# Inverse square roots of the normalizations: ScalarE's Sqrt replaced by a bit-pattern start and three Newton steps on VectorE

## The reference

```
h = layernorm(x) * (1 + ca) + sa;   x = x + ga * mixer(h)
h = layernorm(x) * (1 + cb) + sb;   x = x + gb * experts(h)
layernorm(x) = (x - mean) / sqrt(var + 1e-5)          # over the 256 features
```

## Time and profile before

| | |
|---|---|
| median of 3 runs | 2297.69 us (2289.25 to 2305.37) |
| the profiled execution's own time | 2296.97 us |
| its span in the profile | 2295.2 us |
| PE busy | 1986.1 us, 87% |
| VectorE busy | 1700.5 us, 74% |
| ScalarE busy | 1461.2 us, 64% |
| GpSimd busy | 973.7 us, 42% |
| mean granted TensorE clock | 0.93 of full speed |

### The profile page before, as it was taken

The page is one execution under the profiler, slowest core; times in us unless marked ns, Lnnn a source line. Parts: engine busy times, 40 slices in busy tenths (PEclk is TensorE's granted clock), DMA queues, the critical chain, the costliest instruction groups (busy, mean ns, idle before and its releaser), DMA issues.

```text
span 2295.2 us, 40993 instructions
## 1 busy us (share of the span) xinstructions
PE 1986.1 (87%) x12211; PEld 1622.4 (71%) x12211; DVE 1700.5 (74%) x3913; ACT 1461.2 (64%) x3983; POOL 973.7 (42%) x1025
## 2 busy tenths in 40 slices
PE   4787988887699468999998998999989999689995
PEld 4566766666677256888877887878877788467772
DVE  4676766676634667999899998999989997664444
ACT  1473747465244157888887888878887887345550
POOL 0120302021177112455454765547655567177550
PEclk8799989899699779999999999999999999899998
DMA  4147383837833403444343554445534452635557
GB/s 129 38 152 295 130 350 106 338 109 282 328 97 102 147 10 138 158 154 145 127 147 125 169 175 144 142 137 171 165 137 142 146 179 93 214 117 176 162 146 272
DMA packets 143589, 372.67 MB, mean 162 GB/s; under 512 B 22256, under 2 KB 67696, under 8 KB 141072
## 3 DMA queue, kind: packets, MB, share of 16 engines
q1 hardware_dynamic: 128160, 328.39, 41.8%
q0 software_dynamic: 15216, 41.67, 5.3%
HBM read 232.71 MB, written 137.27 MB: 161 GB/s over the span
## 4 chain that ended last, share of the span: by engine, by line
PE 60%; DVE 17%; ACT 13%; issue 5%; DMA 2%; POOL 1%; SPq 1%; DVEq 0%; POOLq 0%; ACTq 0%
PE bank L2148 12%; PE bank L2204 6%; ACT work L701 5%; PE bank L2585 5%; PE bank L2176 4%; DVE cv L2315 3%; PE bank L2197 3%; PE bank L2189 3%; PE bank L1074 3%; PE bank L2622 2%; ACT l_mat L2239 2%; PE bank L2162 2%; DVE nmax L607 2%; PE bank L1103 2%; PE bank L775 1%
## 5 line engine op out<-in xcount | busy, mean ns | idle before, releaser
L2148 PE MATMUL bank<-h_hi,wi 128*128 128x512 f32 x1024 | 403.9, 436 | 1.3 <-ACTq L151 1.3
L2239 ACT ACTIVATE l_mat<-l_mat,cum_tok 128x128 f32<-128x128 f32 x1024 | 315.1, 424 | 0.0
L2315 DVE SCALAR_TENSOR_TENSOR cv<-bank,cw,cv 128x511 f32<-128x511 f32 (+2 forms) x384 | 287.4, 748 | 32.1 <-ACT cv L2245 13.5
L2368 POOL TENSOR_TENSOR xdec<-xdt,dec_tok 128x384 f32<-128x384 f32 x128 | 107.9, 843 | 387.6 <-DVE xdt L2305 354.4
L2383 POOL TENSOR_TENSOR yg<-yd,sgt 128x512 f32<-128x512 f32 x128 | 227.2, 1775 | 45.7 <-DVE yd L2322 45.7
L2204 PE MATMUL bank<-wo,yg 128*128 128x256 f32 x1024 | 242.5, 380 | 1.5 <-POOL yg L2383 1.5
L2148 PEld LDWEIGHTS bank<-h_hi,wi 128*128 128x128 f32 x1024 | 195.5, 191 | 62.0 <-issue 23.8
L2148 PE MATMUL bank<-h_lo,wi 128*128 128x512 f32 x512 | 203.4, 397 | 0.0
L2204 PEld LDWEIGHTS bank<-wo,yg 128*128 128x128 f32 x1024 | 185.1, 191 | 21.5 <-POOL yg L2383 1.9
L2376 POOL TENSOR_TENSOR gates<-gates,sq 128x512 f32<-128x512 f32 x128 | 164.1, 1282 | 72.0 <-ACT sq L2256 71.9
L845 POOL CAST w_hi<-w_raw 128x512 fp32r<-128x512 f32 x32 | 21.1, 659 | 392.0 <-ACTq L151 241.2
(11 more groups left out here) (419 smaller groups left out, 4947.6 us busy)
## 6 DMA issues: line engine op xcount, KB each, us to landing
sorted_rows<-blank SPq DMA_DIRECT2D x16, 4644.0 KB, 31.9
wi<-in_weights_split SPq DMA_DIRECT2D x128, 512.0 KB, 3.8
l_mat<-running_sums SPq DMA_DIRECT2D x128, 512.0 KB, 4.9
experts_got<-chosen_rows SPq DMA_DIRECT2D x32, 512.0 KB, 8.6
wo<-out_weights_normed SPq DMA_DIRECT2D x128, 128.0 KB
experts_xt<-sorted_rows SPq DMA_DIRECT2D x127, 129.0 KB, 2.3
w_raw<-in_wi SPq DMA_DIRECT2D x32, 256.0 KB, 2.7
in_weights_split<-w_hi SPq DMA_DIRECT2D x32, 256.0 KB, 2.9
```

Source lines behind the costliest of these rows:

```text
L2148: mm = e.matmul(dst[:, :], l, r[:, k, tok], start=(n == 0), stop=(n == 3 * KD - 1))
L2239: last = e.activation(part, part, ACT.Relu, bias=cum_tok[:, c, hh, bass.ds(w.g, 1)], scale=-1.0)
L2315: e.scalar_tensor_tensor(out=cv[:, w.two, n:SEQ], in0=PSX[w.two][:, 0:SEQ - n], scalar=cw[:, bass.ds(w.f, 1), TAPS - 1 - n], in1=cv[:, w.t ...
```

## The change

The wait for ScalarE goes from all five places, with the semaphores for it; `Sqrt` goes from ScalarE, and the two Exps into `warm`. `rsqrt_dve` reads plane 0 as an integer, multiplies it by -0.5 and adds a constant, which gives a first approximation of the inverse root as a bit pattern, and refines it three times with three instructions each: ten dependent instructions where there were five.

```
-        v.e.tensor_scalar(rs[:, 0, 0:TT], mv[:, 0:TT, 1], EPS, None, ALU.add).then_inc(n_var, 1)
-        v.e.wait_ge(n_root, c)
+        v.step(v.e.tensor_scalar(rs[:, 0, 0:TT], mv[:, 0:TT, 1], EPS, None, ALU.add))
         rsqrt_dve(v, TT)
...
     def rsqrt_dve(v, n):
 
-        v.step(v.e.reciprocal(rs[:, 2, 0:n], rs[:, 1, 0:n]))
-        v.step(v.e.tensor_tensor(rs[:, 3, 0:n], rs[:, 0, 0:n], rs[:, 2, 0:n], ALU.mult))
-        v.step(v.e.tensor_tensor(rs[:, 3, 0:n], rs[:, 3, 0:n], rs[:, 2, 0:n], ALU.mult))
-        v.step(v.e.tensor_scalar(rs[:, 3, 0:n], rs[:, 3, 0:n], -0.5, 1.5, ALU.mult, ALU.add))
-        v.step(v.e.tensor_tensor(rs[:, 2, 0:n], rs[:, 2, 0:n], rs[:, 3, 0:n], ALU.mult))
+        v.step(v.e.tensor_scalar(rs[:, 2, 0:n].bitcast(I32), rs[:, 0, 0:n].bitcast(I32), -0.5, ROOT_BITS, ALU.mult,
+                                 ALU.add))
+        for _ in range(3):
+            v.step(v.e.tensor_tensor(rs[:, 3, 0:n], rs[:, 0, 0:n], rs[:, 2, 0:n], ALU.mult))
+            v.step(v.e.scalar_tensor_tensor(out=rs[:, 3, 0:n], in0=rs[:, 3, 0:n], scalar=-0.5, in1=rs[:, 2, 0:n],
+                                            op0=ALU.mult, op1=ALU.mult))
+            v.step(v.e.scalar_tensor_tensor(out=rs[:, 2, 0:n], in0=rs[:, 3, 0:n], scalar=1.5, in1=rs[:, 2, 0:n],
+                                            op0=ALU.add, op1=ALU.mult))
 
     def norm_act(a, b, layer, first=None, last=None):
...
-        a.e.wait_ge(n_var, c)
-        a.e.activation(rs[:, 1, 0:TT], rs[:, 0, 0:TT], ACT.Sqrt).then_inc(n_root, 1)
...
     def route_act(a, r, s, at):
         e = a.e
-        if (s, at) == (0, "m"):
-            e.wait_ge(*q_var(r + 1))
-            e.activation(rs[:, 1, 0:TT], rs[:, 0, 0:TT], ACT.Sqrt).then_inc(q_root.sem, 1)
-            e.activation(warm[:, 1:2], ones_c[:, :], ACT.Exp)
...
-            e.tensor_scalar(rs[:, 0, 0:TT], mv[:, 0:TT, 1], EPS, None, ALU.add).then_inc(q_var.sem, 1)
+            v.own.add(e.tensor_scalar(rs[:, 0, 0:TT], mv[:, 0:TT, 1], EPS, None, ALU.add))
         if (s, at) == (0, "z"):
-            e.wait_ge(*q_root(r + 1))
+            e.wait_ge(s_dve, v.own.now())
             rsqrt_dve(v, TT)
...
-        e.wait_ge(t_var, b + 1)
-        e.activation(rs[:, 1, 0:TT], rs[:, 0, 0:TT], ACT.Sqrt).then_inc(t_root, 1)
-        e.activation(warm[:, 0:1], ones_c[:, :], ACT.Exp)
...
                         ALU.add).then_inc(t_var, 1)
-        e.wait_ge(t_root, b + 1)
+        e.wait_ge(t_var, b + 1)
         rsqrt_dve(v, TT)
```

More of the change, by code:

```diff
@@ L33 @@
 NEG = -3.0e38
+ROOT_BITS = float(0x5F3759DF)
 SSM_HEADS, SSM_P, SSM_N = 64, 64, 128
@@ L186, in program @@
     block = ctx.enter_context(nc.Block())
-    n_var, n_root, n_rows, n_turned, n_high, n_full = (
-        sem("norm_" + n) for n in ("variance", "root", "rows", "turned", "high", "full"))
+    n_rows, n_turned, n_high, n_full = (
+        sem("norm_" + n) for n in ("rows", "turned", "high", "full"))
     def norm_dve(v, b, layer, before=None, meanwhile=None, last=None):
@@ L948, in experts @@
         after = {what: n + 1 for n, what in enumerate(steps_of)}
-        (s_var, s_root, s_route, s_rows, s_turned, s_ht, s_back, s_rowed, s_tw, s_value, s_weighed, s_table) = [signal(n, count) for n, count in (
-             ("variance", 1), ("root", 1), ("routing_handed_on", len(steps_of)), ("rows", GROUPS), ("turned", GROUPS), ("modulated", KD * GROUPS),
+        (s_route, s_rows, s_turned, s_ht, s_back, s_rowed, s_tw, s_value, s_weighed, s_table) = [signal(n, count) for n, count in (
+             ("routing_handed_on", len(steps_of)), ("rows", GROUPS), ("turned", GROUPS), ("modulated", KD * GROUPS),
              ("turned_back", NT // 2), ("rows_back", NT // 2), ("weights_of_top", 1), ("slots", 2 * TOP),
@@ L1127, in act @@
             e = a.e
-            e.wait_ge(*s_var(1))
-            e.activation(rs[:, 1, :], rs[:, 0, :], ACT.Sqrt).then_inc(s_root.sem, 1)
             for b in range(GROUPS):
@@ L1216, in dve @@
             e.wait_ge(s_dve, v.own.now())
-            e.tensor_scalar(rs[:, 0, :], mv[:, :, 1], EPS, None, ALU.add).then_inc(s_var.sem, 1)
-            e.wait_ge(*s_root(1))
+            v.step(e.tensor_scalar(rs[:, 0, :], mv[:, :, 1], EPS, None, ALU.add))
             rsqrt_dve(v, NT)
@@ L1441, in program @@
     sq = sb("sq", [P, SEQ], where=stream)
-    warm = sb("warm", [P, 2], where=stream)
     mod_row = gates[:, 0, 0:2, :]
@@ L1456, in program @@
     h32_of = (h32, outs[:, 2:4, :])
-    p_var, p_root, p_rows, p_turned, p_high = [signal(n, count) for n, count in (
-        ("variance", 1), ("root", 1), ("rows", GROUPS), ("turned", GROUPS), ("modulated", KD * GROUPS))]
+    p_rows, p_turned, p_high = [signal(n, count) for n, count in (
+        ("rows", GROUPS), ("turned", GROUPS), ("modulated", KD * GROUPS))]
     (p_full, p_low, g_wb, g_proj, g_dt, g_bias, g_abs, g_log, g_taps,
@@ L1466, in program @@
             "sums_turned", "bc_products", "sums_split", "last_sums", "dt_projected", "decays", "start_out", "products_masked")]
-    (q_var, q_root, q_rows, q_turned, q_ht, q_route, q_rowed, q_tw, q_slot, q_meta) = [signal(n, count) for n, count in (
-        ("variance", GROUPS), ("root", GROUPS), ("rows", GROUPS), ("turned", KD * TT * GROUPS),
+    (q_rows, q_turned, q_ht, q_route, q_rowed, q_tw, q_slot, q_meta) = [signal(n, count) for n, count in (
+        ("rows", GROUPS), ("turned", KD * TT * GROUPS),
         ("modulated", KD * TT * GROUPS), ("routing_handed_on", 4 * GROUPS + 4), ("rows_back", GROUPS),
@@ L1801, in start_act @@
         e.activation(a_neg[:, :], a_neg[:, :], ACT.Exp).then_inc(g_wb, 1)
-        e.wait_ge(*p_var(1))
-        e.activation(rs[:, 1, :], rs[:, 0, :], ACT.Sqrt).then_inc(p_root.sem, 1)
         def high(b):
@@ L1895, in start_dve @@
         e.wait_ge(s_dve, v.own.now())
-        e.tensor_scalar(rs[:, 0, :], mv[:, :, 1], EPS, None, ALU.add).then_inc(p_var.sem, 1)
-        e.wait_ge(*p_root(1))
+        v.step(e.tensor_scalar(rs[:, 0, :], mv[:, :, 1], EPS, None, ALU.add))
         rsqrt_dve(v, NT)
@@ L2026, in program @@
          "squares", "squares_summed", "out")]
-    s_ones, s_evac, s_zeroed, t_var, t_root, s_tailed = [sem("mix_" + n) for n in (
-        "squares_total", "out_kept", "squares_zeroed", "tail_variance", "tail_root", "tail_done")]
+    s_ones, s_evac, s_zeroed, t_var, s_tailed = [sem("mix_" + n) for n in (
+        "squares_total", "out_kept", "squares_zeroed", "tail_variance", "tail_done")]
     reached["mix_out"] = NB + BACK
```

## The result

| | before | after |
|---|---|---|
| median | 2299.26 us (2289.25 to 2305.37, 6 runs) | 2311.07 us (2306.92 to 2312.11, 6 runs) |
| profiled execution's own time | 2296.97 us | 2311.94 us |
| its span | 2295.2 us | 2310.1 us |
| mean granted TensorE clock | 0.933 | 0.928 |

The ratio after to before is 1.0052, with a 95% interval of 1.0029 to 1.0074: 6.7 to 17.0 us slower, about half a per cent. 2304 was predicted, with a range of 2294 to 2316. The time is inside it, and the likeliest case, slightly slower and within 1%, is the one that came. But the sum was +7.0 us, and the medians differ by 11.8 and the profiled executions by 14.97. Five to eight microseconds are not in the sum.

The account below looks back on a forecast made before the run. No engine was the bound everywhere (TensorE 60% of the chain), so places were priced singly: 2.0 + 0.73 - 1.70 + 5.25 + 0.75 = +7.0 us on 2296.97 gave 2304, range 2294 to 2316.

Parts of the forecast that it names:

- ScalarE's 40 us lie beside other work: 28 table loads and 22 small instructions leave ScalarE, 40 us, nearly all beside VectorE's or TensorE's work.
- ScalarE was on the path: Rival, 5%: the twelve loads at the three mixer boundaries count in full, 15.4 us off, giving 2288.6.
- 2.20 us for a new chain, +0.75: From variance to use, eleven VectorE steps take 2.20 us against 1.45 the old way, 0.75 later if uncovered.
- Attention, 3 x 0.67: In attention groups two to four, TensorE goes on 0.67 us later each, 2.0 together.
- First experts +0.73: In the first experts the chain grows from 1.58 to 2.31 us and TensorE waits for its rows: +0.73.
- Start of the mixer -1.70: At the mixer's start, rows come 1.25 us earlier and the softplus wait loses 0.45: -1.70 together.
- Boundaries 3 x 1.75: At three boundaries between mixer groups, RMS norm costs +0.75 and the routing's root +1.00 each: 5.25.
- Last routing +0.75: In the second experts, 1.45 us becomes 2.20 on VectorE's way to the expert counts TensorE waits for: +0.75.
- The integer instruction: First new VectorE instruction, taken at 0.17 us; rival, 4%: it costs a cast's 1.362, +13 us, 2317.
- The clock, put at 0: TensorE's clock at restarts: 0 in the sum; range from 1.2 us saved to about 5 us lost.
- as much again: Clock allowance for attention and the first experts, equal to the 2.4 us for two more slow boundary restarts.
- The clock stays low for a unit, 2328: Rival, 5%: behind longer boundary holes TensorE stays at 0.50 for a unit, 24 us more, +31 in all.
- The third sign of being wrong: Granted TensorE clocks of 0.5 past the first unit of a mixer group would show the forecast wrong.

Follow-up runs that it names:

- six-step kernel: The changed kernel with six Newton steps instead of three, nine more VectorE instructions in each chain: 2325.41 us, ratio to before 1.013.
- two-step kernel: The changed kernel with two Newton steps instead of three, three instructions less in each chain: 2298.19 us, ratio to before 1.0006.
- filling the hole: The changed kernel with three matmuls of zeros in front of attention's transposes, where TensorE waits: 2310.22 us, ratio to before 1.0061.
- the fillers: Zero-product matmuls in TensorE's waits in the first experts and behind mixer boundaries; before with them 2291.6 us, the kernel with the new root at the mixer's start only 2289.78.

## Why the prediction was right, point by point

- *ScalarE's 40 us lie beside other work:* right. Its wait in the unit behind the boundary grew by 5.26 us when the loads went, and putting all 28 back left the time where it was. The rival "ScalarE was on the path", 2288.6, is refuted.
- *2.20 us for a new chain, +0.75:* right, 2.18 measured, +0.73; for 16 tiles 2.31, to the hundredth.
- *Attention, 3 x 0.67:* the transposes came 2.65 us behind the variance, 1.92 before, so 0.73 each. Right for the chain alone; the clock added about 4 us to it.
- *First experts +0.73:* the chain is right. The stretch measured 219.5 us on average over four executions with the three-step root there, and 215.8 over five with the old (211.9 to 218.1): +3.8, of which 3.1 are not chain.
- *Start of the mixer -1.70:* with the +0.75 of the first boundary's RMS norm -0.95 for the stretch; measured -1.2 and -1.1. The two details, 2.31 us and no wait before `dt_t`, came as written. In the kernel with this root alone the two details came too, but the stretch was 0.1 us shorter and no more, so that -1.70 is the chain's share and not a gain that each kernel gets.
- *Boundaries 3 x 1.75:* the two chains measured 0.73 and 0.97. The three stretches of the groups behind were to add 4.5; they added -0.5 + 3.3 + 2.7 = 5.5. That the sum is so near is in part luck: the second group came 2.2 us under its chains and the third and fourth 1.6 and 1.7 over theirs, and by as much the second and third also differ between kernels that both have the old root there (275.93 and 272.75, 272.91 and 275.93 us). The six-step kernel confirms the rate with +3.74 for 3.6.
- *Behind the last group 0:* right; 0.81 us of cover is left.
- *Last routing +0.75:* the chain came (1977.11 to 1979.29, 2.18 us), and TensorE's wait behind it grew from 10.97 to 11.71 us. The stretch doesn't show it: 335.0 us before, 334.9 and 333.2 after.
- *The integer instruction:* 0.179 us; that rival is refuted.
- *The clock, put at 0:* this is the term that was mis-sized. It was said to have both signs, with -1.2 to about +5, and it came out near the upper end. By the medians it is 11.8 - 7.0 = 4.8 us. The ratio's interval, 6.7 to 17.0 us, doesn't exclude 0, but for attention the kernel with the new root there alone does. The mistake was to price it by the holes behind the boundaries. The restart behind the second boundary did take 2.81 us where before took 1.60, which is 1.2 of the third group's 1.6 us over its chains, and behind the first it was cheaper, 2.33 against 2.80. But the first of these came with the old root in the mixer too (2.83, attention alone), so it isn't the longer hole that makes it. The most came in attention (about 4 us) and the first experts (about 3), which together had been given "as much again". The chain of waits of the changed kernel, behind the first and the second boundary:

```profile
1167.49 2.33 PE bank L2138 x6
...
1442.92 2.81 PE bank L2138 x6
```

- *The clock stays low for a unit, 2328:* didn't come. From 1176 to 1184 TensorE had the full clock, behind the hole of 1.55 us. The third sign of being wrong, clocks of 0.5 past the first unit, could not have told this rival: before has a slow restart far into its second group itself (six matmuls of L2148 in 2.18 us at 1258.30). Stretches, columns as in the earlier trace rows:

```profile
1165.00:1169.00 4.00, 4.00 (x23) 3.05 (x22) 3.89 (x6) 0.63 (x1) 2.44 (x3) 0.50 0.95 374
1176.00:1184.00 8.00, 8.00 (x59) 6.84 (x58) 7.82 (x15) 5.13 (x17) 3.89 (x3) 1.00 0.23 75
```

**What stays open** is what makes the clock fall where it does. Shown is that it costs about 4 us in attention with the three-step root, that work put back on ScalarE doesn't change it, and that a change ahead of a stage moves the slow stretches in it (2.83 and 1.60 us above). Less firm, since each rests on few executions: the two-step kernel had none of it in attention (512.0 us in its one profiled execution), six steps had less than three (513.3, its fastest run), and filling the hole changed nothing. That the time at which TensorE's work starts again decides would fit all of these, but it was only argued: no run shifts a stage by a known time and changes nothing else. The page "TensorE: Matmul & The Clock Gate" of the Trainium skill (section "Part 1: The HAM clock gate") says that the clock follows how busy TensorE has been, and that one kernel can show more or fewer slow matmuls from run to run. The second half agrees with this case (169.26 and 174.93 us for the same 806 matmuls); by the first alone the full stretch of the logits at 0.50 would not be expected.

## What to carry to other kernels

Price a change by who waits for whom at each place: 38 us of one engine's time were worth nothing, and 0.73 to 0.97 us more on another's chain was paid at ten of 14 places, while at the one place where the old producer really was late the rows came earlier. So take such a change only there: the kernel with the mixer's start alone is 5.1 us faster than before, and with the fillers 8.8 us (0.9962, 0.9946 to 0.9979), the lowest median of all. How much of this is the 1.7 us of chain and how much the clock's luck is open. And when a change shifts TensorE's restarts, give the clock a term of its own, of either sign and as large as the same kernel's stretches differ between executions; one profile of each kernel cannot tell it.

## What the runs showed of the hardware that was not expected

- The same kernel's stretches differ by up to 6.2 us (first experts, 211.9 and 218.1) at granted clocks of 0.84 and 0.81, while others (third mixer group) repeat to 0.1 us.
- A stage's slow stretches move when only work ahead of it changes: the third mixer group, with the same instructions in it, took 272.9 us in before and 275.93 with the new root in attention alone; the second took 275.93 in before and 272.75 with the new root at the mixer's start alone.
- Fp32 products of 128x16 (L1018, 32 in 6.85 us) ran at 0.50 of the clock with TensorE busy throughout, after it had had 1.00 shortly in front of them (565.6 to 574.4). In the first execution of before 16 of them took 1.96 us and the last 32 took 5.73. In the changed kernel TensorE was busy in all 15.00 us from 585 to 600, with these products and transposes, at 0.50.
- Integer arithmetic on the bits of a float, with a float factor and a float constant, costs on VectorE what a float instruction does: 0.179 us at 128x4.
- ScalarE went on 0.02 us after the end of a table load, and 28 loads had no price that the total shows.
